# Two transformer layers on one core: every attention unit carries a share of its layer's feed-forward

## What is computed

```
xn = layernorm(x)
x  = x + L0_attn(xn) + L0_ffn(xn)
xn = layernorm(x)
x  = x + L1_attn(xn) + L1_ffn(xn)
```

## Time and profile before

| | |
|---|---|
| median of 3 runs | 662.84 us (662.39 to 664.12) |
| the profiled execution, its span | 661.3 us |
| TensorE busy | 605.0 us (91%) |
| VectorE busy | 411.5 us (62%) |
| ScalarE busy | 298.9 us (45%) |
| GpSimd busy | 183.4 us (28%) |
| mean granted TensorE clock | 0.977 |
| moved by DMA | 88.24 MB |

### The profile page before, as it was taken

How to read it: one execution, slowest core, us unless ns; L and a number is a source line. 1 busy time by engine, 2 the same in 40 slices (tenths; PEclk the granted TensorE clock), 3 DMA queues, 4 the chain that set the end, 5 groups by cost and what they waited for, 6 DMA issues and landing times.

```text
span 661.3 us, 10058 instructions
## 1 busy us (share of the span) xinstructions
PE 605.0 (91%) x3392; PEld 458.7 (69%) x3392; DVE 411.5 (62%) x750; ACT 298.9 (45%) x554; POOL 183.4 (28%) x296
## 2 busy tenths in 40 slices
PE   3778799999988999999989999989989989789997
PEld 2766467577554888888878888747667667458886
DVE  6676976866954444445556565797777686533343
ACT  2215564654636444455644433545444354542331
POOL 7400110121002122212123332335455464621100
PEclk9878899999989999999999999989999999899999
DMA  5679543564439244434343945345344355653321
GB/s 198 172 208 284 143 132 95 129 176 113 125 78 215 90 115 130 127 112 111 112 126 113 234 165 161 82 115 141 113 109 133 113 129 113 155 117 96 96 95 63
DMA packets 39882, 88.24 MB, mean 133 GB/s; under 512 B 4884, under 2 KB 25620, under 8 KB 36760
## 3 DMA queue, kind: packets, MB, share of 16 engines
q1 hardware_dynamic: 31480, 59.29, 33.5%
q0 software_dynamic: 8352, 28.32, 14.4%
HBM read 64.26 MB, written 23.07 MB: 132 GB/s over the span
## 4 chain that ended last, share of the span: by engine, by line
PE 74%; DVE 15%; issue 6%; ACT 3%; DMA 1%; POOL 1%; SPq 0%; DVEq 0%; ACTq 0%; POOLq 0%
PE banks L696 50%; PE banks L752 7%; PE banks L813 6%; DVE neg_max L1097 4%; PE banks L785 3%; PE banks L790 3%; PE banks L757 2%; DVE xn L1039 1%; DVE bn L1016 1%; PE banks L766 1%; DMA big<-q_parts 1%; ACT probs L953 1%; DVE rot_b L1066 1%; DVE o_tok L1113 1%; DVE o_t L1129 1%
## 5 line engine op out<-in xcount | busy, mean ns | idle before, releaser
L1097 DVE TENSOR_REDUCE neg_max<-banks 128x2 f32<-128x512 f32 (+1 forms) x256 | 152.7, 611 | 68.0 <-PE banks L757 36.8
L953 ACT ACTIVATE probs<-banks 128x512 f32<-128x512 f32 (+1 forms) x256 | 131.6, 547 | 95.4 <-PE banks L790 48.7
L696 PE MATMUL banks<-big,w_up 128*128 128x512 f32 x576 | 142.3, 394 | 0.8 <-issue 0.8
L696 PEld LDWEIGHTS banks<-big,w_up 128*128 128x128 f32 x576 | 107.8, 189 | 26.0 <-issue 4.1
L752 PE MATMUL banks<-k_max,big 96*128 96x256 f32 x512 | 109.9, 300 | 13.9 <-DVE neg_max L1097 8.4
L752 PEld LDWEIGHTS banks<-k_max,big 96*128 96x128 f32 x512 | 91.1, 196 | 35.1 <-DVE neg_max L1097 18.2
L696 PE MATMUL banks<-w_down,w_up 128*128 128x512 f32 x384 | 96.7, 394 | 1.6 <-DVE w_up L1153 1.6
L696 PE MATMUL banks<-xnT,w_qkv 128*128 128x256 f32 x576 | 89.1, 297 | 6.0 <-DVE w_qkv L1006 2.9
L696 PEld LDWEIGHTS banks<-xnT,w_qkv 128*128 128x128 f32 x576 | 78.8, 199 | 19.6 <-issue 9.8
L696 PEld LDWEIGHTS banks<-w_down,w_up 128*128 128x128 f32 x384 | 70.2, 188 | 15.6 <-DVE w_up L1006 2.0
L1006 DVE TENSOR_TENSOR w_up<-raw,w_up 128x512 fp32r<-128x512 f32 (+1 forms) x40 | 32.4, 810 | 73.8 <-ACT w_up L884 73.8
(11 more groups left out here) (84 smaller groups left out, 648.5 us busy)
## 6 DMA issues: line engine op xcount, KB each, us to landing
big<-q_parts SPq DMA_DIRECT2D x64, 256.0 KB, 4.3
raw<-in_down POOLq DMA_DIRECT2D x40, 256.0 KB, 2.9
xn_parts<-xnT SPq DMA_DIRECT2D x8, 1024.0 KB, 5.1
q_parts<-stage SPq DMA_DIRECT2D x32, 256.0 KB, 2.5
raw<-in_up POOLq DMA_DIRECT2D x32, 256.0 KB, 3.0
big<-xn_parts SPq DMA_DIRECT2D x16, 512.0 KB, 6.4
raw<-in_attn POOLq DMA_DIRECT2D x10, 512.0 KB, 4.2
k_parts<-stage SPq DMA_DIRECT2D x16, 256.0 KB, 2.7
```

The lines of the kernel that those rows point to most:

```text
L696: mm = nc.tensor.matmul(out_ap, lhs(a), rhs(b_), start=first and j == 0, stop=last and j == 2, **kw)
L953: nc.scalar.activation(probs[:, i, 0:w], banks[:, k % 3, 0:w], ACT.Exp, scale=SCALES[n // B]).then_inc(exp_done, 1)
L1097: nc.vector.tensor_reduce(neg_max[:, s, t, 2 * g:2 * g + 2], banks[:, work_bank(x), :].rearrange("p (r t) -> p r t", r=2)[:, :, 0:w], AX.X ...
```

## The change

There is no feed-forward stretch any more. The list is now `start_order`, 32 times `unit_order`, and `end_order`. A unit has eight slots with its own steps, as before, and between them `spread` lays the fill, by a table of costs: in unit u of layer 0 the two `up` chunks of pair u+1 with their gelus, and the four `down` tiles of pair u; in layer 1 one half of an `up` chunk and one `down` tile. Projections, `wo` and transposes of other batch rows follow behind in the fill, and the `split` steps of a unit all stand at its end. Further:

- A `down` step multiplies a pair of chunks for one token tile in a work bank, and VectorE adds each of these sums to x (64 + 16 additions instead of 16).
- `xnT` is a ring of three batch rows from which both projections and `up` read; the tokens' way through DRAM is gone. One key tile `k_sb` takes the place of two, queries have a ring of three units. `st` has two banks instead of three, `pv` one instead of two.
- Weights come in pieces of 512 instead of up to 1024, in four buffers. The low parts of up and down weights are made by GpSimd, those of attention weights by VectorE. All of layer 0's projections are drained by ScalarE and VectorE (`direct`).
- `mt` is one transpose instead of two, its `mrow` two DMAs instead of one, and it stands in slot 5 (before: slot 2 of 0 to 7). `m` of layer 1 reads only the 128 keys that the first half of the queries may see.
- GpSimd's descriptor memory is 4096 bytes a partition.

```diff
+PIECE = 512
+RAW = 4
+RING = 3
+ST_BANKS = (0, 1)
+WORK_BANKS = (2, 3, 4)
+UP_BANKS = (5, 7)
+PV_BANK = 6
+HID = 4
+HT = 4
+
+COST = {"up": 681, "down": 681, "wo": 693, "qkv": 363, "xn": 440, "v": 220, "st": 233, "m": 250, "mt": 110, "pv": 995}
...
+def downs(L, p, tiles):
+
+    o = []
+    for t in tiles:
+        a = parts(("down", L, p, t))
+        o += a[:1] + ([("add", L, p, t - 1)] if t > tiles[0] else []) + a[1:]
+    return o + [("add", L, p, tiles[-1])]
...
+def start_order():
+    o = [("stats", 0, 0), ("root", 0, 0), ("rstd", 0, 0), ("ln", 0)]
+    o += [("split", 0, "attn", 4), ("split", 0, "attn", 5)] + transposed(0)
+    o += [("split", 0, "attn", 0), ("split", 0, "attn", 1)]
+    o += [("stats", 0, 1), ("root", 0, 1), ("rstd", 0, 1), ("ln", 1)]
+    o += project(0, 2) + [("load_k", 0, 0), ("load_k", 0, 1)]
+    o += [("split", 0, "attn", 2), ("split", 0, "attn", 3)]
+    o += project(0, 0) + [("load_q", 0), ("load_q", 1)]
+    o += transposed(1) + [("split", 0, "up", 0), ("split", 0, "up", 1)]
+    o += project(0, 1) + [("load_q", 2), ("v", 0)]
+    o += parts(("up", 0, 0, 0)) + parts(("up", 0, 1, 0)) + [("hidden", 0, 0), ("hidden", 0, 1)]
+    ms = [("m", 0, i) for i in range(8)] + [("m", 1, i) for i in range(4)]
+    fill = project(1, 2) + project(1, 0) + [("hidden_lo", 0, 0), ("hidden_lo", 0, 1)]
+    o += [x for slot in spread([[m] for m in ms], fill, [1] * len(ms)) for x in slot]
+    k = o.index(("m", 1, 2))
+    o[k:k] = [("mt", 0), ("mrow", 0)]
+    o += [("split", 0, "down", 0), ("split", 0, "down", 1), ("split", 0, "up", 2), ("split", 0, "up", 3)]
...
+    slots = [[("st", u, i)] for i in range(8)]
+    for i in range(8):
+        if i < 4 and u + 1 < UNITS:
+            slots[i].append(("m", u + 1, i + 4))
+        if i >= 4 and u + 2 < UNITS:
+            slots[i].append(("m", u + 2, i - 4))
+    if 0 < u < UNITS - 2:
+        slots[0].append(("load_q", u + 2))
+    if s == 2 and n + 1 < 2 * B:
+        slots[0].append(("load_k", n + 1, 0))
+    if s == 0 and n > 0:
+        slots[0].append(("load_k", n, 1))
+    if u > 0:
+        slots[1].append(("pv", u - 1, 1))
+        slots[2].append(("norm", u - 1, 0))
+        slots[3] += [("norm", u - 1, 1), ("norm", u - 1, 2)]
+        slots[4].append(("norm", u - 1, 3))
+        slots[5].append(("ctx", u - 1))
+    if u + 1 < UNITS:
+        slots[5] += [("mt", u + 1), ("mrow", u + 1)]
+    slots[5].append(("pv", u, 0))
+    if s == 0 and n > 0:
+        slots[2].append(("v", n))
+
+    fill, late = [], []
+
+    if u < LU - 1:
+        p = u + 1
+        cs = (2 * p, 2 * p + 1)
+        fill += parts(("up", 0, cs[0], 0)) + parts(("up", 0, cs[1], 0)) + [("hidden", 0, c) for c in cs]
+        slots[6].append(("hidden_lo", 0, cs[0]))
+        slots[7].append(("hidden_lo", 0, cs[1]))
+    else:
+        c, j = divmod(u - (LU - 1), 2)
+        if c < 2 * CHUNKS[1]:
+            fill += parts(("up", 1, c, j))
+            if j == 1:
+                fill += [("hidden", 1, c)]
+                slots[5].append(("hidden_hi", 1, c))
+                slots[6].append(("hidden_lo", 1, c))
+    if (b, s) in ((0, 0),) and L == 0:
+        slots[3] += [("stats", 0, 2), ("stats", 0, 3)]
+        fill += [("root", 0, 2), ("root", 0, 3)]
+        slots[6] += [("rstd", 0, 2), ("rstd", 0, 3)]
+    if s == 0 and B <= n + 2 < 2 * B:
+        c = n + 2 - B
+        slots[3].append(("stats", 1, c))
+        fill.append(("root", 1, c))
+        slots[7] += [("rstd", 1, c)]
+    if s == 2 and n + 2 < 2 * B:
+        slots[3].append(("ln", n + 2))
+        late += transposed(n + 2)
+    if u < LU:
+        fill += downs(0, u, range(HT))
+    else:
+        q, t = divmod(v - 3, 4)
+        if 0 <= q < CHUNKS[1]:
+            fill += downs(1, q, [t])
+    if s == 0 and n + 1 < 2 * B and n > 0:
+        fill += project(n + 1, 2)
+    if s == 1 and n + 1 < 2 * B and n > 0:
+        fill += project(n + 1, 0)
+    if (s == 2 and n > 0 or s == 0 and n == 0) and n + 1 < 2 * B:
+        fill += project(n + 1, 1)
+    if s == 0 and n > 0:
+        slots[6] += parts(("wo", n - 1, 0))
+    if s == 1 and n > 0:
+        slots[0] += parts(("wo", n - 1, 1))
+    fill += late
+
+    after = []
+    if u < LU - 2:
+        after += [("split", 0, "up", 2 * u + 4)]
+        after += [("split", 0, "up", 2 * u + 5)]
+    if u < LU - 1:
+        after += [("split", 0, "down", 2 * u + 2), ("split", 0, "down", 2 * u + 3)]
+    if u == 0:
+        after += [("split", 0, "attn", 6), ("split", 0, "attn", 7)]
+        after += [("split", 0, "attn", 8), ("split", 0, "attn", 9)]
+    if LU - 6 <= u < LU - 3:
+        k = (2, 0, 1)[u - (LU - 6)]
+        after += [("split", 1, "attn", 2 * k), ("split", 1, "attn", 2 * k + 1)]
+    if u in (LU + 1, LU + 2):
+        k = 6 + 2 * (u - LU - 1)
+        after += [("split", 1, "attn", k), ("split", 1, "attn", k + 1)]
+    if u == LU - 2:
+        after += [("split", 1, "up", 0), ("split", 1, "up", 1)]
+    if u >= LU and v % 2 == 0 and v // 2 < CHUNKS[1] * 2 - 1:
+        after += [("split", 1, "up", 2 * (v // 2) + 2), ("split", 1, "up", 2 * (v // 2) + 3)]
+    if u >= LU and v % 4 == 2:
+        after += [("split", 1, "down", 2 * (v // 4)), ("split", 1, "down", 2 * (v // 4) + 1)]
+    return [x for slot in spread(slots, fill, WEIGHTS[L]) for x in slot] + after
+
+
+WEIGHTS = ((1, 1, 1, 1.3, 1.3, 1, 1, 1), (1, 1, 1, 1.3, 1.3, 1, 1, 1))
+
+
+def end_order():
+    u, n = UNITS - 1, 2 * B - 1
+    o = [("pv", u, 1), ("norm", u, 0), ("norm", u, 1), ("norm", u, 2), ("norm", u, 3), ("ctx", u)]
+    q = CHUNKS[1] - 1
+    o += downs(1, q, [1, 2, 3])
+    return o + parts(("wo", n, 0)) + parts(("wo", n, 1))
+
+
+def program_order():
+    o = start_order()
+    for u in range(UNITS):
...
+def emptied_by(step):
+
+    if step[0] in ("m", "mt", "v", "wo") or step[0] == "qkv" and not direct(step):
+        return step
+    if step[0] == "drain" and (step[1][0] == "xn" or direct(step[1])):
+        return step[1]
+    if step[0] == "add":
+        return ("down",) + step[1:]
+    return None
...
+                if x[0] == "split":
+                    k = sp[x]
+                    if x in lo_pool:
+                        _, to = piece(*x[1:])
+                        pool.wait_ge(hi_split, k + 1)
+                        in_order()
+                        nc.gpsimd.tensor_tensor(to[1], raw[:, k % RAW, :], to[0].bitcast(F32),
+                                                ALU.subtract).then_inc(lo_split_pool, 1)
+                        done[0] = (lo_split_pool, lo_pool[x] + 1)
+                    if k + RAW < len(pieces):
...
+                    w = T if n < B or t == 1 else P
                     for r in range(2):
-                        mm = nc.tensor.matmul(banks[:, k, r * T:r * T + T],
-                                              big[0:ROWS, s, 2 * g + r, t * P:t * P + P], k_max[0:ROWS, 4 * f + g, :],
+                        mm = nc.tensor.matmul(banks[:, k, r * T:r * T + w],
+                                              q_sb[0:ROWS, u % RING, 2 * g + r, t * P:t * P + P], k_sb[0:ROWS, 4 * f + g, 0:w],
                                               start=r == 0, stop=n < B and r == 1, skip_group_check=True)
...
-                    for t in range(TT):
-                        mm = nc.tensor.transpose(banks[0:UH, k, t * P:t * P + P], neg_max[:, s, t, :], ident[:, :])
-                    mm.then_inc(wk_filled, 1)
+                    nc.tensor.transpose(banks[0:TT * UH, k, 0:P], neg_max[:, s, :, :].rearrange("p t h -> p (t h)"),
+                                        ident[:, :]).then_inc(wk_filled, 1)
...
-                    if k >= 3:
-                        pe.wait_ge(exp_done, k - 2)
+                    bank_k = ST_BANKS[k % 2]
+                    if k >= 2:
+                        pe.wait_ge(exp_done, k - 1)
...
+                    for e in mine(range(2)):
+                        c = 2 * p + e
+                        mm = three(banks[:, k, :], lambda h: hid[:, c % HID, h, t * P:t * P + P],
+                                   lambda h: w_down[:, c % 2, h, :], rest > 0 and e == 0, e == 1, skip_group_check=True)
...
+                if adds_to(x):
+                    tile = adds_to(x)[1]
+                    y = x if x[0] == "wo" else ("down",) + x[1:]
+                    dve.wait_ge(wk_filled, wk[y] + 1)
+                    if add_before[x]:
+                        wait_tile_sum(dve, add_before[x])
+                    nc.vector.tensor_tensor(x_res[:, tile, :], x_res[:, tile, :], banks[:, bank_of[y], :],
                                             ALU.add).then_inc(wk_emptied, 1)
...
-    nc = _bacc.Bacc("TRN2", target_bir_lowering=False, num_devices=1)
+    nc = _bacc.Bacc("TRN2", target_bir_lowering=False, num_devices=1, dynamic_dma_scratch_size=4096)
```

809 lines of the change are left out of this document (305 added, 504 removed).

## The result

The changed kernel takes **769.96 us** (768.89 to 772.57, four runs), the kernel before 663.48 in runs beside it: 1.160 times the time, 95% interval 1.156 to 1.164. It is slower, as forecast, but by 107 us and not 34; 697 was forecast, 666 to 734 the range.

The account below looks back on a forecast made before the run. TensorE's work plus its waits was taken as the bound. First `st` at 51, 513.5 of work left, layer stalls 49 and 53, clock 15, small waits 10, tail 4 gave 695.5; with 1.5 on top 697 us, range 666 to 734.

Parts of the forecast that it names:

- exps behind pieces still loading: Layer 0, units 0, 10, 11, 12: more weight pieces than the four buffers, next unit's exps wait; 14.6 us in all.
- weights after 18, 22, 26: Layer 1: ScalarE waits out a projection's rotation before casting up weights; 9.2, 6.6 and 6.9 us lost.
- query chain in 18, 22, 26: Layer 1: queries take 14.1 us through memory, longer than the four slots before `m` reads them; 21.9 us in all.
- the T of the prediction: TensorE's end of a unit, from which the lateness of the next unit's weights is counted.
- the second kind: Layer 1's waits of `m` for queries stored to memory and loaded back; 21.9 us.
- I take nine falls: TensorE's clock falls from 2.4 to 1.2 GHz nine times, 1.7 us of work lost each; 15 us, between 0 and 36.
- Rival C's first half: Each of the 21 stalls brings the clock down, 36 us instead of 15; whole rival 736 us, chance 0.18.
- Prices are the distances between starts in the timeline: TensorE's work priced by distances between instruction starts: 546 us before the change, 537 after.
- 84 us: Old kernel, from the first `st` at 46.6: time beyond TensorE's priced work, all that the new order can win.
- 49 + 53 + 10 + 4: Forecast losses in us: layer 0's stalls 49, layer 1's stalls 53, small waits 10, tail 4.
- Costed at nothing: 64 more VectorE additions hidden behind TensorE, gelu table loads without a wait, smaller descriptor memory; each taken as 0 us.
- Rival B: Stalls serve as each other's cover, 49 + 53 cut to 65, no clock fall; faster, 645 us, chance 0.17.

Follow-up runs that it names:

- The filler: Changed kernel (770) with 202 extra matmuls on TensorE before the twelve up products that wait 1.6 us or more for weights: 759.3 us, 1.145.
- thin additions: Changed kernel (770) with VectorE adding only 64 of 512 columns of each down sum to the residual: 767.4 us, 1.156.
- no tables: Changed kernel (770) with gelu and silu computed as exp, so that ScalarE's table loads between them go: 763.8 us, 1.149.
- the first two experiments: Changed kernel (770) with next unit's up casts behind slot 5: 744.0 us, 1.121; separately, with layer 1's query projections a unit earlier: 770.0 us, 1.158.

## Why the forecast was right in sign and wrong in size

**Where the stalls stand: right in layer 0 place by place, in layer 1 in part.** Idle time of TensorE in the timeline of the changed kernel (a wait for weights is named by the unit whose end makes them, so "unit 13" is the wait at the start of 14):

| place | forecast | measured |
|---|---|---|
| after transposes (units 2, 6, 10) | 2.4 each | 1.7, 1.6, 1.6 |
| after a projection (0, 5, 9) | 2.2 each | 2.1, 2.1, 2.1 |
| after down products (1, 3, 7, 11) | 0.6 each | 0.3 each |
| unit 13, unit 14, unit 12 | 6.9, 10, 1 | 7.0, 10.3, 0.9 |
| exps behind pieces still loading (0, 10, 11, 12) | 6.1, 2.4, 1.1, 5.0 | 5.4, 1.8, 1.3, 5.8 |
| weights after 18, 22, 26 | 9.2, 6.6, 6.9 | 4.7, 6.0, 6.9 |
| query chain in 18, 22, 26 | 7.5, 6.9, 7.5 | 2.8, 5.6, 4.2 |
| exps in layer 1 | none | 2.8, 3.8, 2.2, 2.1, 2.1 |
| row of maxima, four places | 1.4, 1.4, 1.4, 1.2 | 0.4, 0, 0.4, 0.7 |
| masks ahead of `pv` (19, 23, 27) | 3 in all | 0.7 |
| up weights of unit 0, last down weights | none | 5.1, 3.3 |
| `wo` in 16, `m` in 19, last `pv` | none | 3.3, 2.6, 1.4 |

Of the 102 us that were forecast at named places, 77 were measured there, and 29 stood at places that the forecast doesn't name; that the sum behind the first `st` came out at 116 us, forecast and measured, is luck in that part. In layer 0 the method behind it holds: take the last work of a unit on the engine that makes the weights, and add up what stands ahead. The chain of unit 13, from the trace:

```profile
401.79 0.69 DVE rot_b L1010
...
402.51 1.65 DVE rot_b L1012
...
404.18 0.70 DVE rot_b L1016
...
404.91 0.63 ACT stage L884
...
405.60 1.29 POOL stage L651
...
407.02 1.28 POOL w_up L612
```

The projection ended at 400.9 (the T of the prediction), the rounding stands at T + 4.0, the low part lands at T + 7.4. In layer 1 exps that stand behind a rounding or a square root held TensorE up before it came to the query chain: this third kind of wait was missing from the list (13 us), and the second kind measured 12.6 us and not 21.9. That the one shortened the other fits their order in time; no run takes only one of them away.

**The clock: 31 us, the first step that failed.** "I take nine falls", 15 us, was the step. In the records there are 21 stretches at half clock, 136.5 us together, and TensorE was busy for 96 us of them: 48 lost, 46.3 behind the first `st`. There, 28 waits of 1.2 us or more stand beside 20 stretches; waits close together share one, and the waits of 1.60 in unit 7 and of 2.07 in unit 10 brought none. Behind the longest waits a stretch lasted 10 us and not 3.4. Rival C's first half, each stall brings the clock down, came near the truth; its price of 1.7 a fall was too small (2.3 on average). The filler shows that idle time is the cause. The Trainium skill (TensorE: Matmul & The Clock Gate, HAM oscillation) says that waits which come back throttle the engine each time; this case agrees for most waits, with a fall behind the 2.07 us in unit 6, but none behind the same 2.07 in unit 10.

**The work: 39 us, the second step that failed and the larger one.** "Prices are the distances between starts in the timeline" was the step. Behind the first `st` the rest column is 552.6 us and not 513.5. It was the same step for the kernel before: 566.0 us there and not 527, the same 39 short. So of the "84 us" that "are lost there" and are "all the new order can win", 39 were work, 9 the clock, and only 35 idle time. The error has two parts.

*Prices: 17 us.* The distances were taken at their shortest. In unit 5, without a gap, 24 up matmuls take 5.61 us, so 0.234 a matmul of 512 columns and not 0.227; an `m` of 128 keys takes 0.18 and not the 0.12 that I put; the transposes come to 14.6 us and not 6, as `mt` alone takes 0.20, and the masks to 10 and not 14. From 53.8 on the work at these prices, an estimate from the distances in this trace, is 530.1 us.

*Handovers inside the records: 22 us.* At these prices the changed program is 555.2 us; the rest is 582.5. The 27 us between, 0.7 a unit and 4.8 in the start, show as busy. What makes them is not settled: thin additions, no tables or another order leave them as they are.

**The start:** the first `st` at 53.8, forecast 51 (47 to 55). The sum of the errors is 2.8 + 16.6 + 22 + 31 = 73 us (768.4 - 695.5), and the idle time behind the first `st` (115.8 against 49 + 53 + 10 + 4 = 116) adds nothing.

**Costed at nothing:** additions and descriptors rightly, the table loads nearly (6 us of 770). The Trainium skill (ScalarE: Activation LUTs, What ACT_TABLE_LOAD costs) adds a drain of 1.38 us to each switch. This case doesn't agree: in the changed kernel a load starts within 0.02 us of ScalarE's instruction before it, and behind 48 of the 54 the next one starts within 0.02 us (the other six wait for data).

**Rival B** (stalls cover each other) shows only in the first two experiments, where a wait that was taken away let TensorE come sooner to the next. **Where the gain went:** the feed-forward was to fill 84 us, of which 35 were idle time, and 82 us more of idle time than before came as waits, most at the units' ends, with 34 us of half clock behind them. The engines' capacity was not what made them: 112 us were won back by moving steps in the engines' lists, but for one product given from GpSimd to VectorE (3 us). Fewer banks for `st` and `pv` and the single key tile stood in every run after the change, so what they cost is not known.

## What to carry to other kernels

When work is spread into an order that every engine walks in turn, look at the last steps of each piece on the helpers: what is cast, rounded or stored there stands ahead of what TensorE wants next, and a store on a queue holds back the loads behind it that don't need it. Price a stall with its clock: here each us of idle time beyond the kernel before came with 0.4 us lost at half clock. Take work from busy stretches without gaps, not from the shortest distance between two starts, and close the account for the kernel before first; what doesn't add up there is no gain to be had.

## What was not expected of the hardware

- A `tensor_scalar` of VectorE on 128x2 took 4.41 us beside a 5.21 us memset of GpSimd, and its neighbours 0.16; a product of 64x512 took 1.66 instead of 0.69 beside a product of GpSimd (1.77). The Trainium skill (SBUF — State Buffer, Who interferes with whom) has it that some of VectorE's instructions and GpSimd's exclude each other for a whole instruction; the trace agrees.
- Of the 21 stretches at 1.2 GHz ten lasted 3.4 us, four 6.8, six 10.2 and one 13.7. The length doesn't follow the wait alone: 10.2 us with waits of 3.3, 5.1, 5.8, 6.9, 7.0 and 10.3, but 3.4 with one of 5.4 and 6.8 with one of 6.0; two waits of 2.07 us, in units 6 and 10, brought one fall and none.
